# Second node pass with a one-step period: root by step, transposed h2 in the bank of its centered rows, one centering per half; other due counts for the stashes

## The reference, cut to what matters

```python
h = jnp.maximum(_layernorm(x, axis=-1), 0.0)
# layer 0: attention-weighted sum over edges, residual product, batch norm
score = jnp.sum(h[src] * h[dst], axis=-1)
a = softmax of score over the edges of one dst
agg = segment_sum((h @ W_conv + b_conv)[src] * a[:, None], dst)
out = agg + relu(h @ W_res + b_res)
x = x + batchnorm(out) * gamma + beta
# layer 1: message passing
h = jnp.maximum(_layernorm(x, axis=-1), 0.0)
m = gelu(gelu(concat(h[src], h[dst], edge_attr) @ W_m1 + b_m1) @ W_m2 + b_m2)
boxes = segment_sum(m, dst)
c = gelu(concat(h, boxes) @ W_c1 + b_c1)
x = x + h + gelu(c @ W_c2 + b_c2)
```

## Time and profile before

| what | value |
|---|---|
| median of 3 runs | 1614.78 us |
| profiled execution, its own time | 1613.91 us |
| span of the profiled execution | 1612.1 us |
| busy PE / DVE / POOL / ACT | 1289.8 / 1231.4 / 1108.3 / 942.0 us |
| mean granted PE clock, as a share of full speed | 0.869 |
| first edge pass, first DVE operation | 290.73 us |
| second node pass, first transpose of h2 | 692.83 us |
| second edge pass, from 1158.7 us on | 453.4 us |

### The profile page before, as it was taken

How to read it: one execution, slowest core, us unless ns; L and a number is a source line. 1 busy time by engine, 2 the same in 40 slices (tenths; PEclk the granted TensorE clock), 3 DMA queues, 4 the chain that set the end, 5 groups by cost and what they waited for, 6 DMA issues and landing times.

```text
span 1612.1 us, 21905 instructions
## 1 busy us (share of the span) xinstructions
PE 1289.8 (80%) x6227; PEld 786.1 (49%) x6227; DVE 1231.4 (76%) x2432; ACT 942.0 (58%) x1647; POOL 1108.3 (69%) x989
## 2 busy tenths in 40 slices
PE   3566666588778878679989999999849999999982
PEld 2344344377667767544444445444424454454430
DVE  8899997798998998667767677777547777777661
ACT  6599898332332323267777777776526676666651
POOL 7688888777777777777777416767776545455356
PEclk9788888667766766889999999999979999999996
DMA  7577674787864443545556546664645454454410
GB/s 240 182 251 249 221 239 156 249 303 254 296 224 124 140 132 108 202 136 178 187 190 205 174 169 209 212 197 139 208 139 169 131 155 134 144 161 129 124 52 16
DMA packets 141969, 287.34 MB, mean 178 GB/s; under 512 B 33104, under 2 KB 50614, under 8 KB 141852
## 3 DMA queue, kind: packets, MB, share of 16 engines
q1 hardware_dynamic: 109532, 255.32, 47.2%
q0 software_dynamic: 32320, 30.62, 8.3%
HBM read 165.47 MB, written 121.80 MB: 178 GB/s over the span
## 4 chain that ended last, share of the span: by engine, by line
PE 49%; DVE 18%; POOL 12%; issue 9%; ACT 6%; DMA 3%; SPq 2%; DVEq 0%; POOLq 0%; ACTq 0%
PE banks L1512 6%; PE banks L1489 6%; POOL gout L612 5%; POOL x_ring L612 5%; PE banks L1536 4%; PE banks L1418 3%; PE banks L1609 3%; PE banks L1607 3%; PE banks L1616 3%; PE banks L1435 3%; PE banks L1522 3%; DVE sums L844 3%; ACT cT L1239 2%; PE banks L1502 2%; DVE gout L1019 2%
## 5 line engine op out<-in xcount | busy, mean ns | idle before, releaser
L616 POOL DMA_INDIRECT out<-agg,put_last x196 | 198.9, 1015 | 172.8 <-DVE agg L1051 117.8
L612 POOL DMA_INDIRECT agg_ring<-agg_rows,edge_idx x196 | 213.7, 1090 | 131.0 <-DMA edge_agg<-agg_ring 69.5
L612 POOL DMA_INDIRECT x_ring<-in_x,edge_idx x200 | 247.9, 1240 | 73.4 <-issue 63.5
L612 POOL DMA_INDIRECT gout<-in_x,edge_idx x192 | 227.7, 1186 | 58.5 <-issue 57.6
L616 POOL DMA_INDIRECT agg_rows<-agg,put_first x196 | 219.0, 1117 | 59.7 <-issue 57.9
L1374 PE MATMUL banks<-ident,xc 128*128 128x128 f32 (+1 forms) x296 | 58.7, 365 | 103.0 <-DVE xc L772 95.4
L1238 ACT ACTIVATE cT<-banks,packed 96x512 f32<-96x512 f32 (+1 forms) x98 | 66.8, 682 | 112.3 <-PE banks L1512 112.3
L966 DVE TENSOR_TENSOR xc<-banks,xc 128x512 f32<-128x512 f32 (+1 forms) x74 | 51.2, 692 | 98.3 <-PE banks L1536 97.1
L743 DVE TENSOR_REDUCE stat<-sq 128x16 f32<-128x1024 f32 (+1 forms) x98 | 118.7, 1211 | 4.4 <-ACT sq L1224 4.4
L1512 PE MATMUL banks<-hT,packed 64*96 64x512 f32 (+1 forms) x392 | 115.8, 670 | 2.7 <-ACT hT L1231 2.7
L1374 PEld LDWEIGHTS banks<-ident,xc 128*128 128x128 f32 (+1 forms) x296 | 46.8, 188 | 126.5 <-DVE xc L772 96.8
(11 more groups left out here) (195 smaller groups left out, 3427.5 us busy)
## 6 DMA issues: line engine op xcount, KB each, us to landing
xt<-in_x SPq DMA_DIRECT2D x48, 512.0 KB, 6.7
xe<-edge_x SPq DMA_DIRECT2D x96, 256.0 KB, 3.7
agg_rows<-rb SPq DMA_DIRECT2D x48, 512.0 KB
xt<-in_x_t SPq DMA_DIRECT2D x36, 512.0 KB, 5.1
out<-xc SPq DMA_DIRECT2D x36, 512.0 KB, 3.2
r_rows<-rT SPq DMA_DIRECT2D x32, 512.0 KB, 6.6
edge_r<-rr SPq DMA_DIRECT2D x48, 256.0 KB, 4.0
rT<-r_rows SPq DMA_DIRECT2D x24, 512.0 KB, 6.2
```

Of the source, the lines that this page charges most:

```text
L612: A.indirect_dma_start(to, None, table[:, :], bass.IndirectOffsetOnAxis(ap=idx, axis=0), bounds_check=limit, oob_is_err=False).then_inc(si ...
L616: A.indirect_dma_start(table[:, :], bass.IndirectOffsetOnAxis(ap=idx, axis=0), rows_of, None, bounds_check=limit, oob_is_err=False).then_i ...
```

## The change

- **Root by step.** invert_pair becomes invert_step: nine operations on 16 columns for every step instead of on 32 for every second one, nothing placed in the middle. DVE's list now has a period of one step.
- **Transposed h2 in the bank of its centered rows.** transpose_h2 writes to the half of W[s % 2] from which relu_half has read; copy_h2T reads it there; center_x2 of the next step but one waits for that copy. bank(6) is left to transpose_back alone, which waits for the final addition of the half before.
- **One centering in every half**, at the end of PE's list of the half.
- ACT's list and SP's list follow: one square a step, one norm_r a step, one load_r, load_rows and store_final a step.
- **Due counts.** First node pass 9i // 10 instead of 6i // 7 (21 groups at its end instead of 20); first edge pass 4(i + 1) // 3 instead of 6(i + 1) // 5 more per pair; second node pass min(46, 5(s - 22) // 3) by step instead of min(40, 3(i - 12)) by pair.

```diff
-STASH = 12
+STASH = 11
@@ SP, first node pass, then first edge pass
-                due = 6 * i // 7
+                due = 9 * i // 10
-                due = min(G, max(before + 6 * (i + 1) // 5, a + 6))
+                due = min(G, max(before + 4 * (i + 1) // 3, a + 6))
@@ SP, second node pass
+            for s in range(1, S + 3):
+                if is_step(s + 3):
+                    load_r(s + 3)
+                if s == S - 1:
+                    for g in range(4):
+                        load_edges(g)
+                        load_prev(g)
+                        load_attr(g)
+                if is_step(s - 3):
+                    if is_step(s + 5):
+                        load_rows(s + 5)
+                    store_final(s - 3)
+                due = min(46, max(stashed, 5 * (s - 2 * STASH) // 3))
@@ DVE
+            def invert_step(s):
+                c0 = (s % 2) * R
+                invert(s, nodes_of(s), c0, c0 + R, BC_inv, B_ss, s)
...
+            for s in range(1, S + 3):
+                if is_step(s):
+                    sum_x2(s)
+                each((final_half, 2 * s - 5), (add_out, 2 * s - 4))
+                if is_step(s):
+                    invert_step(s)
+                each((relu_half, 2 * s), (relu_half, 2 * s + 1), (final_half, 2 * s - 4), (add_out, 2 * s - 3))
+                if is_step(s + 2):
+                    add_r(s + 2)
@@ ACT
-                A.activation(blocks(hT[:, c], p), blocks(bank(6), p), ACT.Copy).then_inc(B_ht.sem, 1)
+                A.activation(blocks(hT[:, c], p), blocks(W[u // 2 % 2][:, c], p), ACT.Copy).then_inc(B_ht.sem, 1)
...
             for u in range(2 * S + 2):
-                s = u // 2
+                s = u // 2 + 1
+                if u % 2 == 0 and is_step(s):
+                    square_x2(s)
                 if is_half(u):
                     copy_h2T(u)
...
                 if is_half(u - 2):
                     gelu_out(u - 2)
+                if u % 2 == 1 and is_step(s + 3):
+                    norm_r(s + 3)
                 if is_half(u):
                     gelu_c(u)
@@ PE, center_x2
-                B_h.part(pe, s - 2, b + 1)
+                if u >= 4:
+                    pe.wait_ge(B_ht.sem, u - 3)
@@ PE, transpose_h2
-                B_fin.part(pe, (u - 4) // 2, u % 2 + 1)
-                    ins = T.transpose(bank(6)[:, i * P:i * P + p], h2[s % 4][0:p, c:c + P], ident[0:p, 0:p])
+                    ins = T.transpose(W[s % 2][:, c:c + p], h2[s % 4][0:p, c:c + P], ident[0:p, 0:p])
@@ PE, transpose_back
-                if is_half(u + 3):
-                    pe.wait_ge(B_ht.sem, u + 4)
-                else:
+                if u:
                     pe.wait_ge(B_fin.sem, u)
@@ PE, order of a half
                 if is_half(u):
                     transpose_h2(u)
-                if u % 4 < 2:
-                    for k in (u + 4, u + 5) if u % 4 == 0 else (u + 5, u + 6):
-                        if is_half(k):
-                            center_x2(k)
                 if is_half(u - 2):
                     out_product(u - 2)
                 if is_half(u - 3):
                     transpose_back(u - 3)
                 if is_half(u):
                     c_product(u)
+                if is_half(u + 4):
+                    center_x2(u + 4)
```

More of the change, by code:

```diff
@@ L565, in _ @@
                         load_attr(g)
-                for s in (a - 2, b - 2):
-                    if is_step(s):
-                        store_final(s)
-                    if is_step(s + 8):
-                        load_rows(s + 8)
-                due = min(40, max(stashed, 3 * (i - STASH)))
+                if is_step(s - 3):
[3 more added lines that the diff above has]
+                due = min(46, max(stashed, 5 * (s - 2 * STASH) // 3))
                 stash_agg(stashed, due)
@@ L966, in final_half @@
                 V.tensor_tensor(here, bank(6)[0:p, :], here, ALU.add).then_inc(B_fin.sem, 1)
-            for s in range(2):
-                add_r(s)
-            for s in range(2):
-                sum_x2(s)
-            invert_pair(0)
-            for u in range(2):
-                relu_half(u)
-            for s in range(2, 4):
-                add_r(s)
+            add_r(0)
+            add_r(1)
+            sum_x2(0)
+            invert_step(0)
+            relu_half(0)
+            relu_half(1)
+            add_r(2)
             def each(*todo):
@@ L1565, in transpose_r @@
                 if g == 0:
-                    pe.wait_ge(B_h.sem, B_h.after(S - 1))
+                    pe.wait_ge(B_ht.sem, B_ht.after(S - 1))
                 edge_blocks(bank(1), rr[g % 4], edges_of(g)).then_inc(C_rt.sem, 1)
```

45 lines of the change are left out of this document (2 added, 43 removed).

## The result

The changed kernel takes 1574.68 us (median of 4 runs, 1572.49 to 1578.83) beside 1614.11 us for the kernel before (4 runs): ratio 0.9767, 95% interval 0.9750 to 0.9785. The forecast was 1578.

What follows compares the result with a forecast made beforehand. From step 23 POOL's gathers were to hold the second node pass and decide the edge period's start, 35.4 us sooner: 1612.1 - 35.4 = 1576.7 us of span, plus 1.8 around it, 1578. Range 1558 to 1604.

Steps and rivals of the forecast that it cites:

- The pass by itself: Second node pass unheld: PE floor 8.23 us a step, taken as 8.3, if ACT and DVE fit under it.
- ACT's slack: Second node pass, half with the square: copy of transposed h2 ready at 2.05 us, wanted at 2.2; some 0.15 us spare.
- DVE's 7.97: Second node pass: DVE's work in a step, 7.97 us including a root of 2.11, fits with 0.26 us to spare.
- The early cost: End of first node pass: SP waits for group 20, first edge pass 10.5 us late, second node pass at about 702.
- GpSimd's chain: Gathers of agg begin at 889 us, 5.49 us a group under the node pass, 5.24 unhindered.
- rival 4: Denser DVE holds up gathers of agg in the second node pass, 1.73 us each: time 1648 us; chance 0.04.
- The hold from step 23: Second node pass goes at POOL's 9.15 us a step, load of r standing behind stashes; ends near 1138 us.
- The transition: Start of second edge pass: edge_agg waits fall from 22.6 to some 8 us; edge period from 1169, 35.4 us sooner.
- Rival 1: Gathers of agg run without hindrance, 1.31 us each, 5.24 a group: time 1565 us; chance 0.14.
- rival 2: Second node pass misses its period, a step stays at 9.4 us: time 1600 to 1602 us; chance 0.14.
- rival 3: DVE's waits on transposes back stay in the second node pass, 10.0 us a step: time 1636 us; chance 0.05.
- Rival 5: Only the early cost stays, no gain in pace and transition still gated: 1624 us; chance 0.02.

Runs made afterwards that it cites:

- f3: Changed kernel with one more full-width sum of squares a step on DVE, into a row nothing reads: 1579.73 us, ratio 0.9799.
- f1: Changed kernel with transposed h2 back in the bank shared with the transpose back: 1581.75 us, ratio 0.9806.
- f2: Changed kernel with two centerings in every odd half and none in even ones: 1570.89 us, ratio 0.9733.
- f4: Changed kernel with earlier due counts restored in the first two passes, fewer later stashes, load of r a step earlier, ahead of the stash: 1543.55 us, ratio 0.9558.
- e8: The changed kernel itself, unaltered, run where the kernel before takes 2082.91 us: 2048.3 us, ratio 0.9817.

## Why the prediction was right, and by how much

**The pass by itself.** Floor 4.115 us a half, 4.15 measured, 8.30 a step as taken. PE's five pieces of a half are together 0.035 us longer than the chain of the earlier trace rows made them; none of it is waiting. ACT's slack was to be 0.15 us; in the trace the copy ends 0.27 us before the c product starts, which with a hand-over of 0.14 leaves about 0.13. DVE's 7.97 was 7.81 to 7.85 (f3 and DVE's waits). The term that was too big is the root: on 16 columns it takes 1.89 us (810.29 to 812.18 in the trace of the changed kernel) and not the 2.11 of 32 columns, so it is mostly start-up, as assumed, but not all. DVE's slack in a step of 8.3 was thus put at 0.33 us and is 0.46 to 0.49, an error to the safe side. Of the parts, the bank was worth 0.39 us a step (f1) and one centering per half nothing (f2); the prediction did not price them apart.

**The early cost.** 10.5 us were expected for waiting for group 20; DVE's first operation came at 300.43, 9.7 late. The node pass began 6.05 us late where 9.2 were expected (702): of the 9.7, 1.1 came back with the root, about as expected (f4, which has it too but the old counts, needs 400.98 us from one mark to the other where the kernel before needs 402.10), and 2.5 in the edge pass, which had been charged at nothing. f4 starts the edge pass at 292.10 and the node pass at 693.08, so the early counts cost the start of the node pass 5.8 us. They do bring the gathers of agg forward (884.70 against f4's 887.79), of which 1 us is left at the last gather. In the changed kernel, which waits for the gathers anyway, the late start may have cost nothing: without the counts and the rest as it is, it was run only in the other condition.

**GpSimd's chain.** First gather of agg at 884.70 (889 expected), end of the last at 1160.5 (1157). The first term was 4 us too careful: the gathers of x end 6.1 us sooner than before (602.2 and 608.2 us start of the last) instead of 3.5, and next to nothing was lost to a denser DVE, since the scatters took 281.2 us (280.9). The gathers of agg took 275.8 us instead of 268.0: the first 36 groups 200.8 us, 5.58 each instead of 5.49, which makes 4.0 over 45 groups; and behind the pass 16 took 24.8 us (19.6 busy, 5.2 idle), 6.2 a group instead of 5.24, which makes 3.8 over four. The 5.58 isn't an effect of the change. The prediction took 5.49 from twelve gathers in one stretch of 16 us; over all gathers of agg the mean was the same before and after (1090 and 1096 ns busy, and 0.30 us or more between two):

```profile
L612 POOL DMA_INDIRECT agg_ring<-agg_rows,edge_idx x196 | 213.7, 1090 | 131.0 <-DMA edge_agg<-agg_ring 69.5
...
L607 POOL DMA_INDIRECT agg_ring<-agg_rows,edge_idx x196 | 214.8, 1096 | 68.1 <-issue 60.1
```

The Trainium skill, "SBUF — State Buffer", section "Who interferes with whom", lets a DVE operation with two SBUF inputs contend with a GpSimd instruction that reads SBUF. Gathers of 1.00 and of 1.41 us stand next to each other in the trace (1003.57 and 1004.87 us): beside the first DVE has the two relus, which read a bank and a statistic, beside the second the additions of out and r, with both inputs in SBUF. So single gathers agree with it. But their mean in the node pass is 1.085 us (177 gathers) where it was 1.096 (143), though DVE is busy for 84% of the pass instead of 71%, and rival 4's 1.43 busy (1.73 from start to start) did not come: the share of busy time is not what sizes the effect here; the large two-input additions, three a step as before, only come 7% closer together.

**The hold from step 23.** 9.15 us a step were expected. The 23 steps from the sum at 891.02 (step 24) to the last full one at 1106.56 took 215.5 us, 9.37 each: the first four 10.2 each, the other nineteen 9.20, near the 5/3 x 5.58 = 9.30 of the gathers. The pass ends at 1132.8 (1138). The last load of r is issued at 1090.10 and its norm begins at 1095.03, just as worked out (1095), but by then ACT no longer waits for it; from there to the end it takes 37.7 us instead of 43, and these 5 us are not accounted for. That it is the load of r behind the stash, as said, f4 confirms as far as it goes: with it ahead of the stash and gentler counts the hold is gone. f3 shows the other side: a pass slower by 0.63 us a step is hardly held and loses only 4 us, but there the gathers also had a lead of 17 us. So whether the pass is held hangs on how far GpSimd is ahead at step 23 as well as on its pace.

**The transition.** Waits of 8 us were expected and 14.5 measured (11.38 + 3.15). The difference is one term that was not in the sum: the load of group 4, issued at 1144.85, landed 11.8 us later. Loads into that buffer take 3.7 us in the median of the whole run. The period begins at 1171, not 1169, with the load of group 6: the stash of group 48 ended at 1163.0 (1158.6 and 0.4 of issue expected), and from there to DVE's addition it took 7.9 us (9.9 expected). This is the place that the prediction named, but not the only way to it. In the kernel before, the profile's chain runs over the stash; here it runs over the late load of group 4, which by itself brings the load of group 6 to the same moment, 0.2 us after SP's list would have. The prediction named one of two paths that tie.

**Sum.** 1576.7 of span expected, 1577.0 measured; that closeness is luck in part. Along the path that the prediction took for the deciding one, the terms were off by -4.3 us (first gather), +7.8 (gathers), +0.5 (from the last gather to the end of its stash, 2.5 instead of 1.6 + 0.4), -2.0 (from there to the period) and -1.65 (the rest, 406.1 instead of 407.75): they cancel to 0.3. A second path of the same length, through the load of group 4, was not in the sum. PE's terms, off by -3 at the start of the pass and -5 at its end, don't enter at all. Rival 1 (unhindered gathers) failed on 5.58 instead of 5.24 us a group, rival 2 on the 4.15 us half, rival 3 on DVE's wait for the transpose back: 8.0 us in 7 waits from 880 to 1130, and none from 750 to 860. Rival 5 failed on both its conditions: the pass got shorter, and the waits at the transition fell from 22.6 to 14.5 us.

## What to carry to other kernels

When a pass gets faster, look first at what then stands in the in-order queues that serve it: here a good part of what the new list could give (24.6 of 57 us: 464.6 before, 407.4 in f4) was lost while a load waited behind a copy it had nothing to do with, and moving that load and asking for fewer copies gave it back. A transfer that somebody waits for goes ahead of a transfer that waits. And give every part of a change its own run: of three edits named together one was worth 0.39 us a step, one nothing, the third was never undone alone, and the early due counts that came with them started the node pass 5.8 us late. And a pace is better taken as a mean over the whole stage than from one stretch of it: the 5.49 us a group read from sixteen microseconds stood against 5.58 over the pass.

## What was not expected of the hardware

- The kernel before took 2077 to 2083 us on three chips and 1613 to 1614 in the main comparison and beside f1 to f4. In the first condition GpSimd's scatters, where they weren't waiting, went at 1.28 us from one to the next (e8, 800 to 830 us; the mean over all was 1.43 in the kernel before at 1614), while the DMAs moved 68 instead of 198 GB/s and PE, ACT and DVE mostly stood. What makes a chip do that is open; that, in the changed kernel, PE works at 90 of 90 us and at 8.3 us a step in the quiet window after the scatters shows that the engines themselves are not slower there.
- One load of 128 KB at the seam took 11.8 us from issue to landing; the median of its kind is 3.7. It is no single accident: the same load took 12.05 us in f1, 12.09 in f2 and 9.93 in f3. Why is open.
- The first edge pass, delayed by 9.7 us at its start, made up 2.5 of it by its end; its own due counts had changed too, so which of the two brought that is open.
